# Attention scores of a five-engine Trainium2 kernel: three bf16 parts on 64-row halves against two float32r parts on 32-row strips

## What is computed

```python
x = L0_attn_x
x = x + 0.5 * _L0_ffn_ref(_layernorm(x), ...)   # mixture of experts, 8 experts, top 2
x = x + _L0_attn_ref(_layernorm(x), ...)        # 16 heads of 8; keys halved by a convolution; not causal
x = x + 0.5 * _L0_ffn_ref(_layernorm(x), ...)
x = x + 0.5 * _L1_ffn_ref(_layernorm(x), ...)   # causal attention, then 16 experts
x = x + _L1_attn_ref(_layernorm(x), ...)        # causal attention
x = x + 0.5 * _L1_ffn_ref(_layernorm(x), ...)
```

## Time and profile before

| | |
|---|---|
| time, three runs | 1875.72 to 1876.76 us, median 1876.41 |
| profiled execution, span (the page gives no other time for it) | 1910.5 us |
| PE busy | 1556.0 us, 81% |
| DVE busy | 1307.4 us, 68% |
| POOL busy | 1077.0 us, 56% |
| ACT busy | 968.9 us, 51% |
| non-causal stage, first to last unit | about 158 to 410 us |
| causal stage of 32 units | about 542 to 880 us |
| causal stage of 64 units | about 1101 to 1700 us |

### The profile page before, as it was taken

The page is one execution under the profiler, slowest core; times in us unless marked ns, Lnnn a source line. Parts: engine busy times, 40 slices in busy tenths (PEclk is TensorE's granted clock), DMA queues, the critical chain, the costliest instruction groups (busy, mean ns, idle before and its releaser), DMA issues. The chain is left out here.

```text
span 1910.5 us, 46442 instructions
## 1 busy us (share of the span) xinstructions
PE 1556.0 (81%) x17682; PEld 947.9 (50%) x17682; DVE 1307.4 (68%) x3414; ACT 968.9 (51%) x2039; POOL 1077.0 (56%) x1712
## 2 busy tenths in 40 slices
PE   5548888885599998885899499999999999866992
PEld 5432333344355554543677255555555555435772
DVE  7348897883588887766321588888888787775224
ACT  4124667652256676552233166777777766531331
POOL 3436767514467857654354376465566767552552
PEclk9966999987689999886799599999999999975996
DMA  8442323212533222210353343233232223102445
GB/s 279 128 127 86 109 70 95 78 30 83 146 99 115 91 82 78 88 36 22 99 152 102 117 128 105 79 94 103 79 114 82 83 92 103 47 26 62 148 123 160
DMA packets 233187, 188.24 MB, mean 99 GB/s; under 512 B 30035, under 2 KB 221306, under 8 KB 232326
## 3 DMA queue, kind: packets, MB, share of 16 engines
q1 hardware_dynamic: 222582, 166.36, 29.1%
q0 software_dynamic: 10240, 18.89, 3.1%
q10 hardware_dynamic: 144, 0.00, 0.0%
HBM read 104.34 MB, written 80.74 MB: 97 GB/s over the span
## 5 line engine op out<-in xcount | busy, mean ns | idle before, releaser
L1015 DVE TENSOR_REDUCE mx<-PS 128x2 f32<-128x512 f32 (+3 forms) x1408 | 784.3, 612 | 193.2 <-PE PS L653 138.2
L865 ACT ACTIVATE pt<-PS 128x512 f32<-128x512 f32 (+2 forms) x1408 | 669.6, 537 | 311.5 <-PE PS L653 227.9
L670 PE MATMUL PS<-ka,qa 52*128 52x256 bf16 (+3 forms) x2048 | 467.0, 307 | 67.1 <-DVE mx L1015 49.3
L786 PE MATMUL PS<-qa,ka 55*128 55x512 bf16 (+3 forms) x1792 | 462.2, 322 | 33.6 <-DMA qa<-nm 26.5
L730 PE MATMUL PS<-pt,vs 128*32 128x512 f32 (+3 forms) x3584 | 353.1, 484 | 3.7 <-issue 3.0
L653 PE MATMUL PS<-mask_q,identh 64*128 64x64 bf16 x3072 | 301.3, 193 | 0.7 <-issue 0.7
L653 PE MATMUL PS<-mask_k,identh 64*128 64x64 bf16 x3072 | 299.6, 192 | 0.5 <-issue 0.5
L786 PEld LDWEIGHTS PS<-qa,ka 55*128 55x128 bf16 x1792 | 167.6, 94 | 262.6 <-issue 102.7
L653 PEld LDWEIGHTS PS<-mask_k,identh 64*128 64x128 bf16 x3072 | 250.2, 97 | 51.1 <-issue 6.6
L653 PEld LDWEIGHTS PS<-mask_q,identh 64*128 64x128 bf16 x3072 | 254.3, 98 | 30.2 <-issue 8.2
L670 PEld LDWEIGHTS PS<-ka,qa 52*128 52x128 bf16 x2048 | 172.8, 95 | 98.1 <-DVE mx L1015 61.2
(11 more groups left out here) (249 smaller groups left out, 2353.2 us busy)
## 6 DMA issues: line engine op xcount, KB each, us to landing
pt<-in_f_w SPq DMA_DIRECT2D x96, 256.0 KB
qa<-q_parts SPq DMA_DIRECT2D x256, 96.0 KB
ka<-k_parts SPq DMA_DIRECT2D x192, 96.0 KB
q_parts<-parts SPq DMA_DIRECT2D x32, 384.0 KB, 3.0
k_parts<-parts SPq DMA_DIRECT2D x24, 384.0 KB, 2.6
xn<-y_rows SPq DMA_DIRECT2D x32, 256.0 KB, 3.2
hid<-y_rows SPq DMA_DIRECT2D x32, 256.0 KB, 3.5
q_parts<-parts SPq DMA_DIRECT2D x32, 256.0 KB, 3.1
```

The lines of the kernel that those rows point to most:

```text
L670: mm = pe.matmul(PS[:, bank, i * n:(i + 1) * n], k.qa[rows, b % 2, g, h // 2, qb * P:(qb + 1) * P], k.ka[rows, b % 2, g, h // 2, 0:n], sta ...
L786: mm = pe.matmul(PS[:, bank, i * n:(i + 1) * n], k.ka[rows, b % 2, g, h // 2, kb * P:(kb + 1) * P], k.qa[rows, b % 2, g, h // 2, q0:S], st ...
L865: nc.scalar.activation(k.pt[:, u % 2, at[c]:at[c] + len(heads) * n], PS[:, SC_BANK + c % RING, 0:len(heads) * n], ACT.Exp, scale=SCORE_SCA ...
L1015: nc.vector.tensor_reduce(out, PS[:, MX_BANK + t % RING, 0:len(heads) * n] .rearrange("p (h n) -> p h n", n=n), AX.X, ALU.max).then_inc(s. ...
```

## The change

Queries and keys are now split into two float32r parts: a first part rounded to float32r, and the rest. A dimension becomes DROWS = 4 rows, three for the products high by high, high by low and low by high, and one spare, so a head is 32 rows: one **strip** of TensorE's rows, head h of a group on rows 32h to 32h + 31. The spare rows hold zeros on the query side and ones on the key side, written once at the program's start; two of them carry the negated maximum in two parts. `qa` and `ka` hold four-byte elements, one DMA loads each.

- `score_piece` and `max_piece` are matmuls of 32 rows with both operands read as float32r. A head's bank in a causal unit is 512 columns, then 384, then 256 + 128 in one bank (two pieces). Maxima banks are 512, then 384 + 128, then 256.
- A diagonal block's mask is four bf16 products of 32 rows by 32 columns in place of two of 64 by 64. The masks of a slot follow behind both banks' pieces, in turn between score and maxima.
- The maxima run two heads apart from the scores (order 2, 3, 0, 1), so the banks of two neighbouring slots lie on four strips.
- A reduction of the 384 + 128 bank gives four block maxima; a further small one over SBUF joins three of them per head (`mx_ready`).
- `max_split` has two steps for four, `split` two for four, `put_max` two DMAs for three, `write_parts` two for three.
- The step rows, their tables and `steps_landed` are gone.
- `when` moves: max_T behind slot 1, value_p behind 3, x_T, ctx_T and k behind 5, value0 behind 7, v, out and q behind 9, value1 behind 11, o_T behind 5 or 9. The routing work moves by a slot.

```diff
-NPROD = 6
-Q_ROWS = (slice(0, 6, 2), slice(1, 6, 4), slice(3, 4))
-K_ROWS = (slice(3, 6), slice(1, 3), slice(0, 1))
...
+STRIP = P // HG
+DROWS = STRIP // D
+Q_ROWS = (slice(0, 3, 2), slice(1, 2))
+K_ROWS = (slice(1, 3), slice(0, 1))
+SPARE = 3
+MAX_ROWS = (SPARE, SPARE + DROWS)
+WRITES = 2
+MASKS = P // STRIP
...
-        chunks = ([(0, (h,), 512) for h in (0, 1, 2, 3)] + [(1, (h,), 384) for h in (0, 1, 2, 3)]
-                  + [(kb, heads, S - kb * P) for kb in (2, 3) for heads in ((0, 2), (1, 3))])
...
+        chunks = ([(h, ((0, 0, 512),)) for h in heads] + [(h, ((1, 0, 384),)) for h in heads]
+                  + [(h, ((2, 0, 256), (3, 256, 128))) for h in heads])
+        maxes = ([(h, ((3, 0, 512),), 512, 3) for h in other_heads]
+                 + [(h, ((2, 0, 384), (0, 384, 128)), P, 0) for h in other_heads]
+                 + [(h, ((1, 0, 256),), 256, 1) for h in other_heads])
...
+                mm = pe.matmul(PS[:, SC_BANK + c % RING, col:col + n],
+                               k.ka[rows, b % 2, g, kb * P:(kb + 1) * P].bitcast(F32R),
+                               k.qa[rows, b % 2, g, q0:S].bitcast(F32R), start=(i == 0), stop=(last and not causal))
...
+            def slots(u, cs, scores=True, ahead=2):
+
+                more = u + ahead < U
+                for c in cs:
+                    if scores:
+                        score_wait(u, c)
+                        score_piece(u, c, 0)
+                    if more:
+                        max_wait(u + ahead, c)
+                        max_piece(u + ahead, c, 0)
+                for c in cs:
+                    if scores and len(chunks[c][1]) == 2:
+                        score_piece(u, c, 1)
+                    if more and len(maxes[c][1]) == 2:
+                        max_piece(u + ahead, c, 1)
+                for n in range(2 if causal else 0):
+                    for j in range(MASKS):
+                        for c in cs:
+                            if scores and n < len(chunks[c][1]):
+                                score_mask(c, n, j)
+                            if more and n < len(maxes[c][1]):
+                                max_mask(c, n, j)
...
                     if name == "score":
-                        slot(u, n)
+                        slots(u, (n,))
...
+                if causal and t == NMX - 1:
+                    dve.wait_ge(*s.max_taken.at(u * NMX + BLOCK_MAXES))
+                    nc.vector.tensor_reduce(k.mx[:, u % 2, 3, :, 2], k.mx[:, u % 2, 0:3, :, 0].rearrange("p r h -> p h r"), AX.X, ALU.max)\
+                        .then_inc(s.mx_ready.h, 1)
...
+                full, hi, lo = k.nm32[:, u % 2, :], k.nm[:, u % 2, 0, :], k.nm[:, u % 2, 1, :]
+                pool.tensor_copy(hi.bitcast(F32R), full).then_inc(s.nm_hi.h, 1)
                 pool.wait_ge(*s.nm_hi.at(u + 1))
...
+                pool.tensor_tensor(lo, full, hi, ALU.subtract).then_inc(s.nm_ready.h, 1)
...
+                    sp.dma_start(arr[:, b % 2, g, 0:n], scratch[b % 2, g // 2 * 2 * HG:(g // 2 + 1) * 2 * HG, :, 0:n]
+                                 .rearrange("(h n) r t -> n h r t", n=2)[g % 2]).then_inc(s.qk_landed[g].h, 16)
```

More of the change, by code:

```diff
@@ L27 @@
 F32 = mybir.dt.float32
+F32R = mybir.dt.float32r
 BF16 = mybir.dt.bfloat16
@@ L558, in attention @@
+        last_front = (11, 9, 11, 3, 9, 11)
         early, late = ((0,), (1,)), (2, 3)
     else:
[L560 to L564 removed]
@@ L571, in before @@
+    BLOCK_MAXES = max(i for i in range(NMX) if maxes[i][2] == P) + 1 if causal else 0
     def before(u, i, n):
@@ L601, in order @@
         if g == 3 and FIRST + FRONT_LAG <= b < NB - 1:
-            events += [("f_T", b - FRONT_LAG), ("f_l", b - FRONT_LAG)]
+            events += [("f_T", b - FRONT_LAG)]
+        events += [(f"value{i}", u) for i in range(len(early))]
+        if g == 3 and FIRST + FRONT_LAG <= b < NB - 1:
+            events += [("f_l", b - FRONT_LAG)]
         fronts = []
@@ L648, in take_misc, with score_wait @@
                     pe.wait_ge(*misc[0][0].at(misc[0][1]))
-            def mask(bank, col, half, table):
-                for j in range(2):
-                    own = slice(j * HALF, (j + 1) * HALF)
-                    mm = pe.matmul(PS[:, bank, col + j * HALF:col + (j + 1) * HALF],
-                                   k.identh[half * HALF:(half + 1) * HALF, j, :],
-                                   table[half * HALF:(half + 1) * HALF, j, own], start=False, stop=(j == 1))
-                return mm
+            def score_wait(u, c):
+                if c == 0:
+                    pe.wait_ge(*s.m_landed[u % G].at(32 * (u // G + 1)))
+                if before(u, c, NCH) > 0:
+                    pe.wait_ge(*s.pt_ready.at(before(u, c, NCH)))
@@ new lines, in score_piece, with max_piece @@
+                if last and not causal:
+                    mm.then_inc(s.sc_full.h, 1)
+            def max_piece(u, t, i):
+                b, g = u // G, u % G
+                h, pieces = maxes[t][0:2]
+                qb, col, n = pieces[i]
+                rows, last = slice(h * STRIP, (h + 1) * STRIP), i == len(pieces) - 1
+                mm = pe.matmul(PS[:, MX_BANK + t % RING, col:col + n],
+                               k.qa[rows, b % 2, g, qb * P:(qb + 1) * P].bitcast(F32R),
+                               k.ka[rows, b % 2, g, 0:n].bitcast(F32R), start=(i == 0), stop=(last and not causal))
+                if last and not causal:
+                    mm.then_inc(s.max_full.h, 1)
@@ L1008, in max_tile @@
             def max_tile(u, t):
-                qb, heads, n = maxes[t]
+                h, pieces, n, first = maxes[t]
+                groups = sum(piece[2] for piece in pieces) // n
                 dve.wait_ge(*s.max_full.at(u * NMX + t + 1))
@@ L1296, in _ @@
                 load_results(sp, k, i)
-            for half in range(2):
-                row = half * HALF + ROWS
-                sp.dma_start(k.qa[row:row + TB, :, :, :, :].rearrange("r b g s t -> r (b g s) t"),
-                             k.q_steps[:, causal, :].unsqueeze(1).to_broadcast([TB, 4 * G, S])).then_inc(s.steps_landed.h, 16)
             for side in range(2):
@@ L1609, in __init__ @@
         self.xd_ready = new("xd_ready")
[L1610 removed]
+        self.sp_hi = new("sp_hi")
         self.sk_step = new("sk_step")
```

354 lines of the change are left out of this document (157 added, 197 removed).

## The result

The changed kernel takes **2592.8 us** (median of four runs, 2576.1 to 2644.6) where the kernel before takes 1876.6 (four runs, 1875.7 to 1878.3): 1.378 times as long, 95% interval 1.374 to 1.382. It is slower by 716 us; the prediction said 1849 us, with 1960 as its upper end. The ratio is that of the three faster runs; in the fourth, 2644.6 us, the granted clock was lowest (0.618).

A forecast was written before the change was run, and what follows sets the result against it. TensorE was taken to bound the causal units. Causal 0, non-causal -20 and fill -8 gave -28 us on the profiled 1910.5, so 1849 us from the timed 1876.4; own range 1815 to 1880, all but Rival B within 1790 to 1960.

The forecast's parts named there:

- if all four run abreast: Causal slot pairs: score and maxima pieces of two slots overlap on four strips; slots take 3.72 us a unit, against 4.15.
- The sum for a pair: Causal slot pairs: load, pieces and masks of the longest strip, plus 0.10 us for changing between strips and full array.
- Rival B: Every causal pair: the second slot does not pass the first's masks; +2.4 us for 88 units, 2055 us; chance 0.20.
- Masks: Causal slots: a mask of 32 columns takes 0.033 us, bounds 0.015 and 0.034.
- float32r streams once, with a load of 0.11 us: Score and maxima pieces: 512 columns stream in 0.23 us as in bf16, after a weight load of 0.11 us.
- rival C: Causal pairs: a float32r piece streams twice, first masks 0.43 us behind a 512-column piece; +81 us, 1930 us; chance 0.10.
- A pair in 0.55, 0.68 and 0.63 us: Causal unit: times for slots 0/1 and 2/3, then 4/5 and 6/7, then 8/9 and 10/11; sum 3.72 us.
- POOL's and VectorE's parts: Way of the maxima: POOL's four steps, 1.63 us, become two, 0.79; VectorE's added small reduction takes 0.1 us.
- Ring wait: 0.3 us a unit: Causal unit: slot 3 waits for slot 0's bank, three banks in a ring; about 0.3 us, making 8.65 in all.
- Rival D: Causal units: two slots against three banks wait more and starve VectorE; +0.4 us a unit, 1886 us; chance 0.15.
- Non-causal stage: -20 us: Non-causal stage: a shorter way of the maxima removes TensorE's wait, 0.62 us for each of 32 units; bounds 0 and -42.
- Fill: -8 us: Three attention starts: key split loses 1.2 us and the first maxima's way 1.4, so 3 x 2.6 us.

The follow-up runs named there:

- e1_pairs: Changed kernel with the pieces of two neighbouring slots written first and the masks of both behind them; 2013 us, 1.067 times the kernel before.
- e2: Kernel before with every score, maxima and mask product on only the first 32 rows of its half; 1981 us.
- e11: e1_pairs with its pieces read as bf16 from the upper two bytes of each element; 1920 us, 1.024 times the kernel before.
- e3: Changed kernel with its pieces read as bf16 from the upper two bytes of each element, order kept; 2067 us.
- e12: Changed kernel with a block of four float32 products, 128 rows by 512 columns, added behind the first values of each causal unit; 2433 us.
- e13: Changed kernel with a block of ten bf16 products, 128 rows by 512 columns, added behind the first values of each causal unit; 2311 us.
- e14: Changed kernel with all causal masks left out, order of the pieces kept; 1898 us.

## Why the prediction was wrong

**The step that failed first: "if all four run abreast".** The sum for a pair, load + pieces + masks of its longest strip, holds for pieces that the program lists together (0.54 us in e1_pairs). As the changed kernel lists them, pair 0/1 takes 1.13 us. Rival B, with a chance of 0.20, has the mechanism in the main: the second slot doesn't get past the masks of the first. Its unit, 8.65 + 2.4 = 11.05 us, is 0.65 above the 10.4 at the full clock. The evidence was a passing of three instructions, and I let it stand for fourteen. The rule cited for B, of the Trainium skill, that matmuls start and end strictly in program order, isn't what the trace shows either: at 853.20 pieces start ahead of earlier masks. The truth lies between, and the trace of before could not have told where; the right use of it was a larger chance for B.

**The step that was not there: the clock.** Every row of the sum was taken at the full clock, and no rival priced another. Rival B's 2055 us misses by 540: the half clock costs the 600 us above, and B's own price was some 60 too high. The sign was in the rows: the profile before is not at the full clock throughout (0.94 in two stages), and the change cut the rows of each product from 55 to 32 and the masks from 64 rows and columns to 32, twice as many of them. That rows count is shown by e2; that shorter masks do is not.

**What held.**

- *Masks*: 0.033 us each on one strip; measured 0.027 (four in 0.26 us, one being 0.18).
- *float32r streams once, with a load of 0.11 us*: the sum of both is 0.34 as said; rival C, first masks 0.43 us behind, is out.
- *A pair in 0.55, 0.68 and 0.63 us*: in e1_pairs pair 0/1 takes 0.54, 4/5 0.74 (1455.44 to 1456.18), 6/7 0.64 (1457.24 to 1457.88) and 10/11 0.59 (1451.32 to 1451.91). So the arithmetic was right for the order that the change didn't have. e11's full-clock unit is 8.7 us where the sum said 8.65, but that is luck: e11 has no float32r loads, which the sum counts, and waits longer for its banks than the sum does.
- *POOL's and VectorE's parts*: two steps of `max_split` take 0.81 us (0.79 said); the added small reduction takes 0.165 (0.1 said, bounds 0 and 0.42).

```profile
1810.75 0.28 POOL L1186 CAST nm<-nm 16x128 fp32r<-16x128 f32 x1 [13.49 <-ACT nm L925]
1811.11 0.45 POOL L1188 TENSOR_TENSOR nm<-nm 16x128 f32<-16x128 f32 x1
...
L1047 DVE TENSOR_REDUCE mx<-mx 128x4 f32<-128x12 f32 x4 | 0.7, 165 | 0.0
```

**Ring wait: 0.3 us a unit.** Mis-sized. In e1_pairs pair 2/3 takes 1.23 us (1453.43 to 1454.66) for 0.55, so this pair alone waits for 0.7. Slot 3's pieces start at 1454.00 and 1454.13, where the exponential and the reduction of slot 0's banks, begun at 1453.35 and 1453.38, free them. The full-clock unit is 9.2, not 8.65. Rival D had this mechanism, at +0.4 a unit.

**Non-causal stage: -20 us.** Most of the wait went, the time did not. Waits for the maxima to land, at matmuls and weight loads in the window 268 to 388 (against the earlier trace rows):

```profile
PE PS L685 <- DMA qa<-nm: 0.3, 1, 0.3
PEld PS L685 <- DMA qa<-nm: 3.7, 4, 1.2
PE PS L697 <- DVE mx L1043: 3.4, 3, 1.5
```

Of 7.6 and 11.6 us, 0.3 and 3.7 are left; waiting for maxima banks rose from 0.2 to 3.4 us, the stage's clock fell from 0.94 to 0.84, and the stage grew by 5 us. In e11, without float32r, it is 249.0 us, 2 shorter than before. The units that ran wholly at the full clock give a hint: 7.0 us at the median of 13, where the kernel before has 7.7 at the median of 24 and the prediction said 6.9. So the shorter way of the maxima seems to have been worth what was said, and the fall of the clock took it; as the two sets hold different units of the stage, this isn't shown.

**Fill: -8 us.** The first key split fell to 1.16 us from 3.14, 0.79 us more than said, as the first rounding, 1.22 us before, now takes 0.43; but the stretches between the attention stages grew, 132.8 to 140.3 us and 232.3 to 242.4. What lies late there was not looked into.

**What stays open.** Shown: order, float32r and rows each move the clock (e1, e3 and e11, e2), and a dense block of products lifts it though it adds work (e12, e13), whatever its format. That one measure, how much of the array works in a given time, joins them is argued, not shown: six added products that were scattered did nothing, I have only their dilution to explain it, and ten in a block are also more columns. How many instructions a piece can pass isn't measured either: three were passed before, and never all that stand between two slots of the changed kernel. Why e14, with almost nothing but pieces and full-array work, still has 0.93 is not explained.

## What to carry to other kernels

Price a change to small products at both levels of TensorE's clock, and look for the level in every stage of the profile: an engine at 100% busy and a clock of 0.50 is doing half of what its busy share says. Where products lie on different strips, list those that should run abreast next to each other, with the short ones that wait on them behind all of them; here that one choice was worth 580 us, most of it through the clock. When two ways of counting, such as "passes the next three" and "passes none", give 1849 and 2055 us, a row that shows three is no evidence for fourteen.

## What the runs showed of the hardware that I had not expected

- TensorE can be busy almost without a pause and stay at 1.2 GHz: 1083.8 of 1085.7 us at 0.52, in one stretch at 0.50 for 1038 us. The Trainium skill (TensorE: Matmul & The Clock Gate, Part 1) says that activity releases the throttle, and its advice is to avoid idle gaps; the gaps were absent here, and that was not enough.
- Added work can make a kernel faster: ten products of 512 columns in each causal unit, 2593 to 2311 us, in a block; six scattered ones over all 128 rows made it slower by 376 to 440 us.
- Instructions of one strip pass those of another that wait, but only so many: pieces passed masks at 853.20, not the eight of a slot as a whole, in none of 384 pairs.
- A float32r product on 64 rows doesn't run beside a 32-row one on the other half (2700.89 and 2701.62 at the half clock), while four on 32 rows start within 0.01 us, and bf16 products of 55 and 52 rows on the two halves do too. Whether the format or the unequal rows make the difference was not tested.
